# Layer-0 attention in a hybrid two-layer kernel: probability-times-value products issued for two key tiles at a time, with a third exponential buffer

## The reference, cut to what matters

```python
q = _rms(heads(wq), qn_w)
k = _rms(heads(wk), kn_w)
v = heads(wv)
scores = jnp.einsum('bhqd,bhkd->bhqk', q, k) * HD ** (-0.5)
...
scores = jnp.where(causal[None, None], scores, -jnp.inf)
attn = jax.nn.softmax(scores, axis=-1)
ao = jnp.einsum('bhqk,bhkd->bhqd', attn, v).transpose(0, 2, 1, 3).reshape(B, T, C) @ wo.T
```

## Time and profile before

| | before |
|---|---|
| median of 3 runs | 1404.76 us (1403.76 to 1405.98) |
| the profiled execution's own time | 1405.97 us |
| its span | 1404.2 us |
| PE busy | 1298.0 us (92%) |
| DVE busy | 1075.4 us (77%) |
| ACT busy | 765.6 us (55%) |
| slot 5, length | 65.55 us |
| DVE busy in slot 5 | 58.53 us |
| tail, length | 39.81 us |
| granted TensorE clock, whole span | 0.97 of full |

### The profile page before, as it was taken

The page is one execution under the profiler, slowest core; times in us unless marked ns, Lnnn a source line. Parts: engine busy times, 40 slices in busy tenths (PEclk is TensorE's granted clock), DMA queues, the critical chain, the costliest instruction groups (busy, mean ns, idle before and its releaser), DMA issues. The chain is left out here.

```text
span 1404.2 us, 26518 instructions
## 1 busy us (share of the span) xinstructions
PE 1298.0 (92%) x8834; PEld 992.0 (71%) x8834; DVE 1075.4 (77%) x3354; ACT 765.6 (55%) x1657; POOL 327.0 (23%) x458
## 2 busy tenths in 40 slices
PE   4789999999999999979986899899999999999997
PEld 2666767677777777655654677678888888888776
DVE  6888888889898988463247876687777887787776
ACT  6344546455555464634333565566666666666664
POOL 3101111110101010100006166433321233333264
PEclk9699999999999999989997999999999999999999
DMA  2000000000000000010000320202221012220012
GB/s 103 1 1 1 1 1 1 1 1 1 1 1 1 1 1 1 1 46 0 0 0 4 87 71 28 69 1 61 61 61 43 28 53 61 61 61 9 9 33 59
DMA packets 39698, 36.21 MB, mean 26 GB/s; under 512 B 2320, under 2 KB 38160, under 8 KB 39312
## 3 DMA queue, kind: packets, MB, share of 16 engines
q1 hardware_dynamic: 37520, 30.36, 7.2%
q0 software_dynamic: 2048, 4.20, 1.0%
HBM read 26.17 MB, written 8.39 MB: 25 GB/s over the span
## 5 line engine op out<-in xcount | busy, mean ns | idle before, releaser
L1137 ACT ACTIVATE pe_<-PS 128x512 f32<-128x512 f32 (+3 forms) x384 | 175.9, 488 | 140.0 <-PE PS L2196 136.0
L1895 DVE CUSTOM_DVE_ANT_0 PS<-PS,mask_row 128x128 f32<-128x128 f32 (+7 forms) x256 | 194.0, 765 | 49.5 <-PE PS L2346 47.4
L1205 ACT ACTIVATE PN<-PS,NM 128x128 f32<-128x128 f32 (+7 forms) x256 | 189.2, 740 | 76.2 <-DVE NM L1895 44.7
L2353 PE MATMUL PS<-ident,PN 128*128 128x128 f32 x1152 | 176.4, 276 | 11.6 <-DVE pe_ L1903 7.4
L2345 PE MATMUL PS<-KA,QA 128*128 128x512 f32 (+3 forms) x384 | 158.2, 413 | 17.6 <-issue 7.4
L2353 PEld LDWEIGHTS PS<-ident,PN 128*128 128x128 f32 x1152 | 135.6, 141 | 49.5 <-issue 30.2
L2176 PE MATMUL PS<-kta,qta 128*128 128x512 f32 (+3 forms) x384 | 149.7, 416 | 6.3 <-DVE tmqs L1571 2.3
L2196 PE MATMUL PS<-qtb,kta 128*128 128x512 f32 (+3 forms) x384 | 134.1, 388 | 0.9 <-ACT pe_ L1137 0.9
L2346 PE MATMUL PS<-KB,QA 128*128 128x512 f32 (+3 forms) x384 | 129.8, 351 | 0.0
L1571 DVE CUSTOM_DVE_ANT_0 PS<-PS,W 128x128 f32<-128x128 f32 (+3 forms) x256 | 125.0, 495 | 4.7 <-PE PS L2176 3.3
L907 POOL TENSOR_SCALAR_AFFINE_SELECT pe_<-pe_ 128x512 f32<-128x512 f32 x64 | 42.0, 657 | 362.7 <-ACT pe_ L1137 362.7
(11 more groups left out here) (314 smaller groups left out, 2910.5 us busy)
## 6 DMA issues: line engine op xcount, KB each, us to landing
W<-w SPq DMA_DIRECT2D x40, 384.0 KB, 4.1
W<-by_expert SPq DMA_DIRECT2D x10, 256.0 KB, 4.7
expert_out<-YS SPq DMA_DIRECT2D x10, 256.0 KB, 2.3
by_expert<-WOZ SPq DMA_DIRECT2D x2, 1024.0 KB, 6.8
W<-w SPq DMA_DIRECT2D x1, 1728.0 KB, 9.7
W<-w SPq DMA_DIRECT2D x1, 1536.0 KB, 6.0
X<-x SPq DMA_DIRECT2D x2, 512.0 KB, 4.8
out<-X SPq DMA_DIRECT2D x2, 512.0 KB, 3.2
```

Of the source, the lines that this page charges most:

```text
L1137: act.activation(pe_[:, h, n % 2, 0:w], PS[:, 4 + h % 2, 0:w], ACT.Exp, scale=HD0 ** -0.5)\
L1205: act.activation(prob_rows(u, r), scores_of(u), ACT.Exp, bias=NM[:, u:u + 1], scale=-1.0, accum_out=SM[:, r % 2, u:u + 1]).then_inc(score_ ...
L1895: dve.tensor_tensor_reduce(scores_of(u), scores_of(u), mask_row[:, S - w:S], -HD1 ** -0.5, -MASKED, ALU.add, ALU.min, NM[:, u:u + 1]).then ...
L2353: ins = pe.transpose(PS[:, ring_bank[item, r], (j - 4 * k) * P:(j - 4 * k + 1) * P], prob_rows(u, r)[:, j * P:(j + 1) * P], ident[:, :])
```

## The change

Three things are altered. The `pv` steps become six per trip (`NPV`), each doing key tiles 2r and 2r + 1 one after the other, and the step for tiles n - 2 and n - 1 stands behind the scores of tile n. Since three key tiles are then in flight, the exponentials rotate over three places (`prob0`): the two halves of `pe_` and, as the third, `W0[:, W0_FIRST:W0_FIRST + 2048]`, so the load of the first mixture's weights moves behind the end of the attention, in front of layer 1's weights on SyncE's queue. And `SLOT` and `SLOT_TAIL` each lose six letters s; letters t and f keep their order. `SLOT_HEAD` is as it was.

```diff
+        NPV = NB // 2
+        LAST = [1, NPV - 1]
+        def prob0(n):
+            if n % 3 < 2:
+                return pe_[:, :, n % 3, :]
+            return W0[:, W0_FIRST:W0_FIRST + HG * 512].rearrange("p (h n) -> p h n", h=HG)
...
-        for n in range(NB + 1):
-            if n < NB:
-                SECOND0 += [("st", n, h) for h in range(HG)]
-            if n >= 1:
-                SECOND0 += [("pv", n - 1)]
+        for n in range(NB):
+            SECOND0 += [("st", n, h) for h in range(HG)]
+            if n >= 2 and n % 2 == 0:
+                SECOND0 += [("pv", n // 2 - 1)]
             if n == 7:
                 SECOND0 += [("to", 0)]
+        SECOND0 += [("pv", NPV - 1)]
         SECOND0 += [("to", 1)]
...
-            sp.dma_start(W0[:, W0_FIRST:], w0_in[:, W0_FIRST:]).then_inc(mix_loaded, 16)
 
             sp.wait_ge(s0_dve.sem, s0_dve.at(("zt", 1), TRIPS - 1))
             sp.wait_ge(s0_pe.sem, s0_pe.at(("to", 1), TRIPS - 1))
+            sp.dma_start(W0[:, W0_FIRST:], w0_in[:, W0_FIRST:]).then_inc(mix_loaded, 16)
...
-                        if n >= 2:
-                            wait(act, s0_pe, ("pv", n - 2), before)
-                        act.activation(pe_[:, h, n % 2, 0:w], PS[:, 4 + h % 2, 0:w], ACT.Exp, scale=HD0 ** -0.5)\
+                        if n >= 3:
+                            wait(act, s0_pe, ("pv", (n - 3) // 2), before)
+                        act.activation(prob0(n)[:, h, 0:w], PS[:, 4 + h % 2, 0:w], ACT.Exp, scale=HD0 ** -0.5)\
...
+                        for n in (2 * r[1], 2 * r[1] + 1):
+                            c, j = SWEEP_B[n]
...
+                            for h in range(HG):
+                                wait(pe, s0_act, ("ex", n, h), before)
```

More of the change, by code:

```diff
@@ L306, in program @@
         NB = len(SWEEP_B)
-        LAST = [3, NB - 1]
+        NPV = NB // 2
[4 more added lines that the diff above has]
+            return W0[:, W0_FIRST:W0_FIRST + HG * 512].rearrange("p (h n) -> p h n", h=HG)
         LATE_HIGH, LATE_AT = 3, 8
@@ L356, in merge @@
             return order
-        SLOT = merge(("stsftssfffffsstttffstfssfstsffftffffsftftfsstssftfsstftssftfstfftsfsttfsstsfstffffftfffts"
-                 "ftftsssftfsssfstfstfstsffststfsstfstfssftsffstsfstfftsffsstssfsftfssfsstffttfstfffttfstfs"), t=train(1) + train(0), f=FIRST0, s=SECOND0)
+        SLOT = merge(("stsftssfffffsstttffstfssfstsffftffffsftftfstssftfsstftssftfstfftsfsttfstsfstffffftffft"
+                 "sftftsssftfssfstfstfstsffststfsstfstfsftsffstsfstfftsffsstssfftfssfsstffttfstfffttftfs"), t=train(1) + train(0), f=FIRST0, s=SECOND0)
         SLOT_HEAD = merge(("fttftffffffftfffffffftfffftffftfftffftffffffffffffftfftfftfftffftfftfftfftffttfftfftfftfff"
                  "fft"), t=train(0), f=FIRST0)
-        SLOT_TAIL = merge(("ssttssstsstsssstssssstssssstsstsststsssststststssstssssstststsssstssssstssssstssststs"), t=train(1), s=SECOND0)
+        SLOT_TAIL = merge(("ssttssstsstsssstsssstssssstsstststsssststststsstssssstststssstssssstsssstssstts"), t=train(1), s=SECOND0)
         for half, last in ((0, ("st", 3, HG - 1)), (1, ("st", NB - 1, HG - 1))):
@@ L899, in values @@
             def values(trip, b, g):
-                wait(pool, s0_pe, ("pv", NB - 1), trip, 1)
+                wait(pool, s0_pe, ("pv", NPV - 1), trip, 1)
                 pool.tensor_copy(put(tmv, 0), heads(QKV, b, g, 2 * D)).then_inc(s0_values, 1)
@@ L905, in diagonals @@
                     wait(pool, s0_act, ("ex", n, HG - 1), trip)
-                    block = pe_[:, :, n % 2, 0:P]
+                    block = prob0(n)[:, :, 0:P]
                     pool.affine_select(out=block, in_=block, compare_op=ALU.is_ge, fill=0.0, base=0,
@@ L2199, in slot @@
                     elif r[0] == "pv":
[L2201 to L2215, removed]
+                        for n in (2 * r[1], 2 * r[1] + 1):
+                            c, j = SWEEP_B[n]
+                            q0 = max(512 * c, P * j)
+                            if n == 0:
+                                pe.wait_ge(s0_values, before + 1)
+                                wait(pe, s0_dve, ("oc", 1), before, 1)
+                            elif j == 0:
+                                wait(pe, s0_dve, ("oc", 0), before)
+                            if n in DIAG0:
+                                pe.wait_ge(s0_masked, len(DIAG0) * before + DIAG0.index(n) + 1)
+                            for h in range(HG):
+                                wait(pe, s0_act, ("ex", n, h), before)
+                                ins = pe.matmul(PS[32 * h:32 * h + 32, 6, q0 - 512 * c:512],
+                                                tmv[:, j, 32 * h:32 * h + 32], prob0(n)[:, h, 0:512 * (c + 1) - q0],
+                                                start=(j == 0), stop=(j == 4 * c + 3), skip_group_check=True)
                         ins.then_inc(s0_pe.sem, 1)
```

## The result

The changed kernel takes 1435.07 us (median of 4 runs, 1432.44 to 1437.03) where the kernel before takes 1404.38 us in the same series (1403.76 to 1405.98): a ratio of 1.022, 95% interval 1.0201 to 1.0239, so 30.7 us slower. The forecast was 1420.2 us, and the time lies above its range of 1406 to 1429.

What follows compares the result with a forecast made beforehand. Slots were taken as bound by meshing VectorE and TensorE lists, despite TensorE's 92% busy: 1405.97 + 15.1 (seven slots) + 0.3 (tail) = 1421.4, less 1.2 for the median, 1420.2 us; range 1406 to 1429.

Steps and rivals of the forecast that it cites:

- TensorE's saving: Each joined `pv` pair saves TensorE some 0.32 us, 15.4 us in all; rival that this shows as faster time: chance 0.13.
- The loads of the second tile: Strip weight loads of a pair's second tile taken as hidden; by the skill's rule the sum would be some 5 us higher.
- place (1): `zc` 2 to `y` 2 of `train(0)`, which gets tiles 6 and 7: `y` 0.64 us later, loss 0.55 us.
- The three places: `zc` 2 to `y` 2 of `train(0)` and of `train(1)`, `y` 3 to `ds` 3: losses 0.55, 0.5, 0.5 us a slot.
- The other three pairs: Tiles 2 and 3, 4 and 5, 10 and 11, thought mostly covered: 0.2 us each, bounds 0 and 0.55.
- I take 0: Gaps emptied of a `pv` give back nothing; TensorE's time there turns into waits for sl and `mx`.
- It never waits longer: ScalarE's exponential of tile n waits no longer than for that tile's scores, so the third buffer costs nothing.
- A slot: Sum over six pairs, 0.55 + 0.5 + 0.5 + 3 x 0.2: 2.15 us longer per slot, 15.1 us over seven.
- three open gaps: Upper case in which all three open gaps cost 0.55 us: a slot loses 3.2 us, time near 1430 us.
- The tail: Stage after the slots: 1.9 us saving taken back by uneven gaps; +0.3 us, bounds -1.9 and +2.2.
- signs named ahead: Profile: x16 groups of 1.87 us, gaps 2.5 and 2.8, VectorE hole 0.4 to 0.6 before L1474, busy 58.5 per slot.
- place (2): `zc` 2 to `y` 2 of `train(1)`, which gets tiles 0 and 1: 2.55 us against 2.00, loss 0.5 us.

Runs made afterwards that it cites:

- one pair alone: Kernel before with three buffers and only tile 6's `pv` moved down next to tile 7's, between `zc` 2 and `y` 2 of `train(0)`: 1409.68 us, ratio 1.0032.
- the first run: Kernel before in its own order with single `pv` steps, but three places for the exponentials and the late load: 1403.85 us, ratio 0.9997.
- the copy late: Changed kernel with VectorE's copy of bank 6 (second half's output) put back behind the last `dc`, the pair staying ahead of `y` 4: 1433.15 us, ratio 1.0199.

## Why the prediction was wrong

*TensorE's saving, right.* Two tiles of 512 columns take 1.85 us, forecast 1.87; a cut costs 0.29 us, forecast 0.32. The loads of the second tile are hidden as forecast (the 0.16 us in the earlier trace rows are the whole time of the eight loads; they start within less): at place (1) they stand at 423.96 and 424.39, inside the x16 group.

```profile
423.96 0.13 PEld L2221 LDWEIGHTS PS<-pe_,arena 128*32 128x32 f32 x4 [0.30 <-issue]
424.39 0.13 PEld L2221 LDWEIGHTS PS<-pe_,arena 128*32 128x32 f32 x4 [0.30 <-issue]
```

By the rule of the Trainium skill, "TensorE: Matmul & The Clock Gate", section on what overlaps and what doesn't, a pair would have taken some 1.97 us by my estimate; the trace has 1.85 and disagrees.

*The three places, right.* Forecast 0.55, 0.5 and 0.5, measured 0.64, 0.51 and 0.49 us. `y` or `ds` was the last to come, and VectorE could not catch up, except behind the third, where `ds` 3 to `dc` 3 gave back 0.29 of 0.78.

*The other three pairs, mis-sized.* Forecast 0.2 each, with bounds 0 and 0.55. Tiles 10 and 11 came to 0.21, through the copy of bank 6 as said: its run took 0.3 of a slot back. Tiles 4 and 5 came to 0.45, the 0.86 up to `ds` 0 less the 0.41 behind it. Tiles 2 and 3, between `dc` 3 and `zc` 4 of `train(1)`, cost 0.65, beyond the bound, and nothing came back behind them. I had taken a place without a training wait as covered; `zc` 4 was as much on the chain as `y`. For these two pairs no run moved the pair alone.

*Every step but the pairs, put at nothing: the first step that failed.* "I take 0" for what the emptied gaps give back was right: what the gap ahead of `y` 1 gave back, 0.28 us, was gone again at `dc` 1, in the changed kernel and with one pair alone. But the sum of a slot has terms for the six pairs only, and so puts every other step at nothing. The change takes letters out of the string and so shifts which steps of the second sweep stand ahead of which training step. `to` 0 slid ahead of `y` 1, and with it VectorE's division ahead of the chain: 0.49 us a slot, 3.5 us in all by its run. The order of the two kernels had this in it; I looked only at the pairs.

*"It never waits longer" for the third buffer, true of ScalarE and beside the point.* The buffers are free, as the first run shows. But the prediction asked only what ScalarE waits for. With fewer `pv` among them, TensorE's score steps run into their own two banks, and wait for ScalarE. In a slot this costs little of its own: moving the score steps brought nothing there, and halving the exponentials 0.2 us. In the tail it costs some.

*A slot, 3.63 us instead of 2.15.* The difference of 1.48 is 0.49 for `to` 0, 0.71 for the other three pairs (0.65 + 0.45 + 0.21 against 0.6), 0.09 for the three places, and small ones. Slots 4 to 6 stand at 68.9 to 69.2 us, forecast 67.7. The prediction's own upper end for a slot, 3.2 us, needs 0.55 at all six pairs and not at the "three open gaps" that it names; the slots came to 3.4 on average. Slots 1 to 3 lost 3.2, 3.1 and 3.3 us, so their late VectorE work did cover a part, against what was forecast.

*The tail, +5.92 instead of +0.3, failed.* The bound of 2.2 was one slot's loss, and the 3.7 us beyond it are more than half of the 6.1 by which the time lies above the range. But the tail has no first sweep: its fillers are score steps and `pv` alone, and the score steps can run only two ahead of ScalarE. So it has no other work to put in the place of a `pv` that is taken away, and a pair that stands in a short stretch between two training steps is in the chain in full: +1.62 us from `dc` 2 to `zc` 3, +0.74 from `y` 4 to `ds` 4, +0.93 from `ds` 4 to `dc` 4. From `zc` 4 to `y` 4, with two tiles as before but none any more between the scores of tiles 9 and 10, it is +0.98, half of which went when a score step was moved. Two stretches from `zc` to `y` that lost their `pv` grew by 0.96 and 0.47 us, by waits for exponentials; a third fell by 0.20, to 2.00. This split is read from the rows. The runs show parts of it: one pair at a time, with the other steps as before, tiles 10 and 11 cost the tail 0.76 us, tiles 8 and 9 another 1.41, and tiles 6 and 7 took 0.25 off; 0.7 us go when score steps are moved and 1.0 with shorter exponentials. For tiles 0 to 5, the larger part, no run dealt the tail anew, and that part of the cause stays open.

Of the signs named ahead, the x16 group and the gaps of 2.5 and 2.8 us came, and VectorE's loss of 0.57 at place (1) too. It does not show as one hole of 0.4 to 0.6 us ahead of L1482: the rows have 0.30 us at place (2), and at (1) 0.20 ahead of the first-sweep piece and 0.14 behind it. VectorE's busy time in slot 5 did not stay at 58.5 but is 59.59.

The sum by measured terms is 23.7 us of slots and 5.9 of tail, 29.6, against 15.4 forecast: 8.6 of the difference of 14.2 are the slots, 5.6 the tail.

## What to carry to other kernels

When a hand-written order is changed, compare the whole lists and not only the steps that the change is about: price each step that has changed sides with a step of the critical chain, on every engine that walks through that order. A step that looks costly may be what fills a wait; before it is taken out of a gap, ask what TensorE will run into next there, whether the stretch behind takes back what the gap gives, and whether the stage has other work to put in. And bound the cost in a stage from the resources of that stage, not from its neighbour's.

## What the runs showed of the hardware

Three things that I had not expected. A cut of a run of strip products by one full-array product costs 0.29 us beyond that product's own time (12.2 us over 42 cuts; the product at place (1) takes 0.26 us to the next start). And ScalarE's exponential of 256 columns takes 0.38 us and of 512 columns 0.60 where its record stands alone, so halving the work takes a third off its length, and a stage bound by the order of its lists, as the tail is, hardly sees even that. And the same two waits of TensorE, 0.88 and 0.45 us, were followed in one profile, that with the copy late, by a stretch at the lower level of the granted clock (0.50), which made `y` 1 to `ds` 1 1.47 us longer, and in that of the changed kernel by none.
